# A four-layer attention and time-mix kernel: the steps of the four compute engines placed in another order

## The chip, the core and the metric

The kernel runs on one core of a Trainium2 chip. Its compute engines are TensorE (PE in the profile; its weight loads stand in rows of their own as PEld), VectorE (DVE), ScalarE (ACT) and GpSimd (POOL). SyncE (SP) issues the transfers. Each engine works through its own list of instructions in order and waits at semaphores for what the others make. The metric is the device time of one execution, in microseconds (us), as the median of three runs.

## The reference

`x` has 16 sequences of 128 tokens with 256 channels, and there is a context of the same shape. Four layers follow each other, and each takes the output of the one before:

```python
x = _L0(ctx, x, mask0)    # 16-head attention of x over [ctx, x] (256 keys), RMS norm, 256->1024 GELU ->256
x = _L1(x, ctx, mask1)    # 32-head attention over ctx with 8 kv heads, output product, layer norm
x = _L2(x, state)         # time-mix: token shift, low-rank mixes, then for each of 32 heads of 8x8:
                          #   out = r @ (faaaa * k v^T + s);  s = k v^T + w * s   over 128 tokens
                          # group norm, gate, and a channel-mix of three 256x256 products
x = _L3(x, ctx, mask3)    # 16-head attention of ctx over the layer-normed x, gated output product
```

All of it is in float32.

## The kernel before

The 16 sequences are handled in eight turns of two. The layers of neighbouring turns overlap: the program has phases `@start`, `@first`, `@second`, `@steady0` to `@steady4`, `@closing`, `@last` and `@end`, and a steady phase holds layer 0 of one turn, layers 3 and 2 of the turn before it, and layer 1 of its own turn at the end.

Which engine does which step when is not decided by the code of the steps. Four tables of text, `PE_ORDER`, `ACT_ORDER`, `DVE_ORDER` and `POOL_ORDER`, list the steps of an engine one after the other, and the engine's program walks through its table. A step like `u0`, `q1` or `m2` is one product of 256 channels on PE (L702 and L712) and, on another engine, the emptying of its PSUM bank. `aT`, `yT`, `x1T` are turnings of activations (L693, on PE) and their copies to SBUF.

An attention is cut into jobs of 512 columns: `turn0.7` is the eighth job of layer 0. For each job PE makes the scores of four jobs at once (L757, step `scores`), DVE adds the mask and takes the maximum (L1241), ACT exponentiates (L1064, step `exps`), PE turns the result with four transposes into a PSUM bank (L768, step `turn`), ACT (layers 0 and 3, L1051) or DVE (layer 1, L1257) copies the bank to the buffer `ET`, and PE multiplies that with the values (step `weigh`, L792 for layers 0 and 3, which takes two jobs at once, and L800 for layer 1). A weigh uses PE as four column groups of 32, while turns, products and transposes use the whole array.

Buffers are few. The bank that a turn or a product writes is one of a ring of three (`BANKS = 3`), `E` has two places and `ET` four. So the copy of a job waits for the weigh of the job four before it, by a line in `copy_turned` (L1051 and L1257 stand behind it):

```python
if g >= 4:
    act.wait_ge(sems["pv"], turn("pv", g - 3))
```

The time-mix has a scan over the tokens in eight parts, `vr0` to `vr7`. For each part PE spreads the values (`vp0`, `vp1`), POOL seeds it (`kv<-s,wP`, L1633, step `vr` of POOL_ORDER), DVE multiplies (L1477) and scans (L1484, step `vr` of DVE_ORDER), POOL multiplies with the receptance (`Z`, L1623, step `gather` of POOL_ORDER), and after four such parts PE gathers them (L830, `gather3` and `gather7`). Scan states have two places and `Z` four:

```python
pool.wait_ge(sems["scan"], turn("scan", u - 1))          # seed of part u, from u = 2
dve.wait_ge(sems["z"], turn("z", u - 1))                 # scan of part u, from u = 2
pool.wait_ge(sems["gathered"], turn("gathered", (v - RING_Z) // 4 * 4 + 4))   # Z of part v, from v = 4
```

Of the kernel before, what the change touches and what calls it, by code (L numbers as in the profile page):

```python
# [64 lines left out]
@start xT cT q0 k0l k0c v0c k1 v0l @first aT @start v1 @first scores0.0 turn0.0 turn0.1 scores0.4 turn0.2 weigh0.1  # L65
turn0.3 scores0.8 weigh0.3 cT turn0.4 turn0.5 turn0.6 turn0.7 scores0.12 weigh0.5 turn0.8 weigh0.7 turn0.9 turn0.10
weigh0.9 turn0.11 turn0.12 turn0.13 weigh0.11 turn0.14 turn0.15 weigh0.13 sum0 weigh0.15 o0 nT u0 u1 u2 u3 m2 x1T q1
scores1.0 xT q0 k0l turn1.0 scores1.4 turn1.1 k0c weigh1.0 turn1.2 turn1.3 weigh1.1 v0c weigh1.2 turn1.4 scores1.8
turn1.5 turn1.6 weigh1.3 v0l turn1.7 weigh1.4 weigh1.5 turn1.8 scores1.12 turn1.9 weigh1.6 turn1.10 k1 weigh1.7
turn1.11 weigh1.8 weigh1.9 turn1.12 turn1.13 weigh1.10 weigh1.11 weigh1.12 @second scores0.0 @first turn1.14 turn1.15  # L70
weigh1.13 weigh1.14 @second turn0.0 @first sum1 weigh1.15 v1 @second scores0.4 turn0.1 turn0.2 @first o1 @second
weigh0.1 turn0.3 turn0.4 weigh0.3 scores0.8 turn0.5 turn0.6 turn0.7 scores0.12 weigh0.5 turn0.8 k3 xaT weigh0.7
turn0.9 turn0.10 v3 t turn0.11 mw weigh0.9 turn0.12 turn0.13 mk mv d1 weigh0.11 weigh0.13 k2 v2 turn0.14 turn0.15 d2
sum0 weigh0.15 mr mg o0 r2 vp0 aT g2 nT bonus u0 u1 u2 cT vp1 u3 gather3 m2 gather7 x1T yT q1 xT scores1.0 ynT q0 o2
turn1.0 k0l turn1.1 scores1.4 weigh1.0 k0c xcT weigh1.1 turn1.2 turn1.3 scores1.8 v0c turn1.4 weigh1.2 fk weigh1.3
turn1.5 turn1.6 fr turn1.7 fv weigh1.4 turn1.8 scores1.12 x4T weigh1.5 turn1.9 weigh1.6 weigh1.7 turn1.10 weigh1.8
weigh1.9 q3 turn1.11 weigh1.10 turn1.12 v0l weigh1.11 turn1.13 turn1.14 @steady0 scores0.0 @second weigh1.12 weigh1.13
k1 turn1.15 weigh1.14 sum1 weigh1.15 v1 @steady0 turn0.0 @second o1 @steady0 turn0.1 turn0.2 scores0.4 turn0.3
weigh0.1 turn0.4 weigh0.3 turn0.5 scores0.8 turn0.6 turn0.7 weigh0.5 turn0.8 scores0.12 turn0.9 weigh0.7 turn0.10 xaT
# [5 lines left out]
turn1.12 weigh1.9 weigh1.10 v0l x4T weigh1.11 turn1.13 turn1.14 q3 k1 turn1.15 @steady1 scores0.0 @steady0 weigh1.12
weigh1.13 weigh1.14 sum1 weigh1.15 @steady1 turn0.0 @steady0 o1 @steady1 turn0.1 scores0.4 turn0.2 turn0.3 @steady0 v1
@steady1 weigh0.1 turn0.4 turn0.5 scores0.8 weigh0.3 turn0.6 turn0.7 weigh0.5 turn0.8 scores0.12 turn0.9 xaT weigh0.7
turn0.10 turn0.11 weigh0.9 turn0.12 scores3.0 t turn0.13 weigh0.11 mw mk turn0.14 weigh0.13 d1 mv k2 turn0.15 turn3.0
mr mg v2 turn3.1 d2 scores3.4 sum0 weigh0.15 r2 turn3.2 g2 turn3.3 o0 weigh3.1 vp0 turn3.4 bonus turn3.5 weigh3.3
turn3.6 weigh3.5 k3 nT turn3.7 u0 weigh3.7 u1 sum3 vp1 u2 gather3 u3 o3 m2 gather7 v3 aT yT x1T q1 cT ynT scores1.0 xT  # L90
o2 q0 k0l turn1.0 turn1.1 weigh1.0 scores1.4 turn1.2 xcT k0c weigh1.1 weigh1.2 turn1.3 turn1.4 scores1.8 v0c fk
weigh1.3 turn1.5 weigh1.4 turn1.6 fr fv turn1.7 turn1.8 weigh1.5 v0l scores1.12 turn1.9 x4T weigh1.6 weigh1.7 turn1.10
weigh1.8 weigh1.9 turn1.11 q3 turn1.12 @steady2 scores0.0 @steady1 turn1.13 weigh1.10 turn1.14 weigh1.11 k1 turn1.15
weigh1.12 weigh1.13 weigh1.14 sum1 weigh1.15 v1 @steady2 turn0.0 @steady1 o1 @steady2 turn0.1 scores0.4 turn0.2
turn0.3 weigh0.1 turn0.4 turn0.5 scores0.8 weigh0.3 turn0.6 weigh0.5 turn0.7 turn0.8 scores0.12 xaT turn0.9 weigh0.7
turn0.10 turn0.11 weigh0.9 scores3.0 turn0.12 turn0.13 t weigh0.11 weigh0.13 mw mk turn0.14 d1 mv turn0.15 d2 k2 v2
turn3.0 mr mg scores3.4 turn3.1 r2 sum0 weigh0.15 turn3.2 turn3.3 o0 g2 weigh3.1 turn3.4 turn3.5 bonus weigh3.3 vp0
weigh3.5 nT k3 turn3.6 turn3.7 u0 u1 u2 vp1 weigh3.7 sum3 u3 v3 gather3 m2 gather7 o3 aT yT x1T q1 cT ynT xT scores1.0
o2 q0 k0l turn1.0 scores1.4 turn1.1 turn1.2 k0c xcT weigh1.0 weigh1.1 weigh1.2 turn1.3 v0c turn1.4 scores1.8 fk
turn1.5 fr turn1.6 fv weigh1.3 weigh1.4 turn1.7 turn1.8 scores1.12 x4T weigh1.5 turn1.9 weigh1.6 weigh1.7 turn1.10  # L100
weigh1.8 weigh1.9 q3 turn1.11 turn1.12 v0l weigh1.10 weigh1.11 turn1.13 turn1.14 @steady3 scores0.0 @steady2 k1
turn1.15 weigh1.12 weigh1.13 weigh1.14 sum1 weigh1.15 @steady3 turn0.0 @steady2 o1 @steady3 scores0.4 turn0.1 @steady2
v1 @steady3 turn0.2 turn0.3 weigh0.1 turn0.4 weigh0.3 turn0.5 turn0.6 scores0.8 weigh0.5 turn0.7 turn0.8 scores0.12
xaT turn0.9 weigh0.7 turn0.10 weigh0.9 turn0.11 scores3.0 turn0.12 turn0.13 t weigh0.11 turn0.14 mw mk mv turn0.15
weigh0.13 turn3.0 k2 sum0 d1 v2 weigh0.15 d2 turn3.1 mr mg scores3.4 turn3.2 r2 turn3.3 o0 g2 weigh3.1 turn3.4 turn3.5
vp0 bonus nT weigh3.3 turn3.6 k3 turn3.7 u0 u1 weigh3.5 weigh3.7 sum3 u2 vp1 u3 gather3 v3 m2 gather7 o3 yT aT x1T q1
cT ynT scores1.0 xT q0 o2 turn1.0 turn1.1 scores1.4 turn1.2 k0l k0c turn1.3 xcT weigh1.0 weigh1.1 weigh1.2 turn1.4
scores1.8 turn1.5 v0c turn1.6 weigh1.3 weigh1.4 fk fr weigh1.5 fv turn1.7 turn1.8 weigh1.6 x4T scores1.12 turn1.9
turn1.10 weigh1.7 turn1.11 q3 weigh1.8 turn1.12 weigh1.9 turn1.13 k1 v0l weigh1.10 turn1.14 weigh1.11 weigh1.12
# [1651 lines left out]
```

## Time and profile before

| | us |
|---|---|
| median of three runs (1122.0 to 1125.25) | 1123.47 |
| span of the profiled execution | 1119.7 |
| PE busy, 7776 matmuls | 973.4 (87%) |
| DVE busy | 817.1 (73%) |
| ACT busy | 733.0 (65%) |
| POOL busy | 256.2 (23%) |

The profile is of one execution, whose span is 3.8 us under the median of the runs. Five steady turns of some 126 us each make up the middle; start and tail are emptier. A busy time says how long an engine ran instructions, not whether the others waited for it: for that one reads the chain of waits that ended last, and the idle time ahead of a line with what released it.

### The profile page before, as it was taken

To read this page: it belongs to the slowest core of one execution; us is meant where nothing else is said; L and a number is where in the kernel's file an instruction comes from. 1 tells how busy PE (TensorE), PEld (TensorE's weight loads), DVE (VectorE), ACT (ScalarE), POOL (GpSimd) and SP (SyncE) were. 2 spreads that over 40 slices of the span, in tenths; PEclk is the share of its full clock that TensorE was granted. 3 is DMA by queue.
4 is the path that set the end of the run, shared out by engine and by line. 5 is a ranking of instruction groups with operands and counts; after the bars stand their busy time and mean duration, and the time that the engine had idled before them with its cause. 6 is when DMAs were issued, how large, how long until landed. Compare 5 with 4: busy or idle time off the path is not lost.

```text
span 1119.7 us, 23998 instructions
## 1 busy us (share of the span) xinstructions
PE 973.4 (87%) x7776; PEld 700.2 (63%) x7776; DVE 817.1 (73%) x3119; ACT 733.0 (65%) x2663; POOL 256.2 (23%) x349
## 2 busy tenths in 40 slices
PE   6779898999989899999989899989989899878365
PEld 4456566667767577756766576656766577555243
DVE  3608768977878776987878677977878687876624
ACT  2629852888568883898477882888658883882115
POOL 3210314121411332131411413031321313120300
PEclk9989999999999999999999999999999999899568
DMA  8100000000010001000010001000010000000000
...
DMA packets 18667, 18.90 MB, mean 17 GB/s; under 512 B 7280, under 2 KB 16752, under 8 KB 18288
## 3 DMA queue, kind: packets, MB, share of 16 engines
...
## 4 chain that ended last, share of the span: by engine, by line
PE 47%; ACT 14%; DVE 13%; issue 7%; POOL 2%; DMA 0%; DVEq 0%; POOLq 0%; ACTq 0%
PE ring L702 10%; PE ring L712 10%; ACT E L1064 9%; PE ring L768 8%; PE psS L757 4%; DVE SS L1484 3%; PE ring L933 2%; DVE S L1241 2%; PE psO L800 2%; PE ring L693 2%; PE psO L792 2%; POOL Z L1623 2%; DVE kv L1477 1%; PE psO L830 1%; PE ring L923 1%
## 5 line engine op out<-in xcount | busy, mean ns | idle before, releaser
L1064 ACT ACTIVATE E<-S,nmax 128x128 f32<-128x128 f32 (+1 forms) x1024 | 423.6, 418 | 33.1 <-PE ring L768 22.1
L1241 DVE CUSTOM_DVE_ANT_0 S<-psS,mb 128x128 f32<-128x128 f32 (+1 forms) x1024 | 261.8, 319 | 30.5 <-PE psS L757 15.1
L702 PE MATMUL ring<-slot,w_l 128*128 128x256 f32 x992 | 244.2, 393 | 18.2 <-ACT slot L1025 14.6
L768 PE MATMUL ring<-ident,E 128*128 128x128 f32 x1280 | 200.0, 286 | 45.4 <-ACT E L1064 35.6
L702 PEld LDWEIGHTS ring<-slot,w_l 128*128 128x128 f32 x992 | 185.9, 195 | 57.5 <-ACT slot L1025 17.3
L768 PEld LDWEIGHTS ring<-ident,E 128*128 128x128 f32 x1280 | 142.9, 143 | 120.3 <-ACT E L1064 79.1
L1064 ACT ACTIVATION_READ_ACCUMULATOR E<-S,nmax 128x1 f32 x1024 | 195.7, 191 | 0.0
L712 PE MATMUL ring<-w_l,slot 128*128 128x256 f32 (+1 forms) x640 | 151.6, 381 | 10.9 <-DVE slot L1505 3.5
L712 PEld LDWEIGHTS ring<-w_l,slot 128*128 128x128 f32 x640 | 114.4, 194 | 37.3 <-issue 7.5
L1257 DVE COPY ET<-ring 128x512 f32<-128x512 f32 x140 | 93.2, 685 | 31.9 <-PE ring L768 31.5
L1051 ACT ACTIVATE ET<-ring 128x512 f32<-128x512 f32 x180 | 100.3, 588 | 21.2 <-PE ring L768 20.1
L1484 DVE TENSOR_TENSOR_SCAN SS<-wP,kv 128x258 f32<-128x258 f32 x128 | 105.4, 863 | 5.7 <-POOL Z L1623 3.6
L757 PE MATMUL psS<-keys,slot 32*128 32x512 f32 (+1 forms) x768 | 95.1, 575 | 11.0 <-DVE nmax L1241 5.6
L1025 ACT ACTIVATE slot<-ring 128x512 f32<-128x512 f32 x72 | 42.6, 594 | 76.0 <-PE ring L693 57.8
L693 PE MATMUL ring<-ident,slot 128*128 128x128 f32 x384 | 63.0, 290 | 27.9 <-DVE slot L1217 7.1
L1623 POOL TENSOR_TENSOR Z<-SS,slot 128x512 f32<-128x512 f32 x64 | 79.1, 1237 | 28.0 <-DVE SS L1484 19.1
L1241 DVE DVE_READ_ACCUMULATOR2_ANT nmax<- 128x1 f32 x1024 | 85.5, 83 | 0.0
L1595 POOL TENSOR_TENSOR keys<-k0T,in 128x512 f32<-128x512 f32 x32 | 32.9, 1040 | 222.2 <-PE psS L757 215.1
L693 PEld LDWEIGHTS ring<-ident,slot 128*128 128x128 f32 x384 | 44.2, 146 | 52.2 <-issue 13.1
L792 PE MATMUL psO<-ET,V 128*32 128x128 f32 x1536 | 64.0, 283 | 4.7 <-ACT ET L1051 3.3
L1633 POOL TENSOR_TENSOR kv<-s,wP 128x4 f32<-128x4 f32 x64 | 13.2, 214 | 203.4 <-ACT slot L1025 130.5
L1441 DVE SCALAR_TENSOR_TENSOR slot<-ring,colt,slot 128x256 f32<-128x256 f32 x80 | 34.9, 478 | 32.8 <-PE ring L933 32.7
...
## 6 DMA issues: line engine op xcount, KB each, us to landing
...
```

Of the source, the lines that this page charges most:

```text
L693: m = pe.transpose(b[:, c, a * P:(a + 1) * P], src[:, a, c * P:(c + 1) * P], ident[:, :])
L702: m = pe.matmul(b[:, a, :], w[:, k, m0 + a * P:m0 + (a + 1) * P], src[:, k, :], start=(k == 0), stop=(k == kt - 1))
L712: m = pe.matmul(b[:, bb, 0:n], src[:, k, bb * P:(bb + 1) * P], w[:, k, :], start=(k == 0), stop=(k == kt - 1))
L757: ins = pe.matmul(psS[m % QUAD][:, x * w:(x + 1) * w], queries, keys[rows, group % RING_K, x * w:(x + 1) * w], start=True, stop=True)
L768: m = pe.transpose(b[:, k, :], E[:, g % RING_E, k * P:(k + 1) * P], ident[:, :])
L792: m = pe.matmul(psO[32 * c:32 * c + 32, t, bb * P:(bb + 1) * P], v[:, window(8 * t + 4 * half + c, half, 16)], e, start=(half == 0 and sbl ...
L1051: act.activation(ET[:, g % 4, :, :], bank(phase, i, turned).rearrange("p a (h s) -> p (a h) s", h=2), ACT.Copy).then_inc(sems["emptied_A"], 1)
L1064: ins = act.activation(E[:, g % RING_E, h * w:(h + 1) * w], S[:, g % RING_S, h * w:(h + 1) * w], ACT.Exp, bias=nmax[:, g % 4, h:h + 1], sc ...
L1241: ins = dve.tensor_tensor_reduce(S[:, g % RING_S, h * w:(h + 1) * w], psS[g % QUAD][:, h * w:(h + 1) * w], bias[:, bb, :], -1.0, HUGE, ALU ...
L1257: dve.tensor_copy(ET[:, g % 4, :, :], bank(phase, i, turned).rearrange("p a (h s) -> p (a h) s", h=2))\
L1484: ins = dve.tensor_tensor_scan(SS[:, u % 2, a, :, :].rearrange("p b t -> p (b t)"), wP[:, ct, :, :].rearrange("p b t -> p (b t)"), kv[:, u ...
L1623: pool.tensor_tensor(Z[:, v % RING_Z, :, :].rearrange("p a (b t) -> p a b t", b=PAIR), SS[:, v % 2, :, :, 0:P], r, ALU.mult).then_inc(sems ...
```

## The change

The four tables are written anew, and nothing else is. The tiles, buffers, transfers, the queue of SP and the bodies of the steps are the same; each engine has the same steps as before in another order, and line numbers behind the tables are two lower (L798 after is L800 before). The diff consists of the tables alone, of which one pair of lines, the end of steady0's scan in `PE_ORDER`, is shown:

```diff
-weigh3.5 turn3.6 u0 turn3.7 u1 vp1 weigh3.7 sum3 u2 u3 gather3 o3 m2 gather7 v3 yT aT x1T q1 cT ynT scores1.0 xT o2 q0
+weigh3.5 weigh3.7 vp1 sum3 u2 u3 gather3 o3 m2 gather7 v3 yT x1T aT q1 ynT cT xT scores1.0 q0 o2 scores1.4 turn1.0 k0l
```

On PE the weighs stand together more often. In the layer 1 attention of steady0, from the transposes ahead of one `scores` on, PE had this (L800 is the weigh of layer 1, four instructions for one job; L768 the turn of a job; L757 scores; L712, L693 and L702 products and transposes of other layers):

```order
L768 MATMUL ring<-ident,E 128x128 x4
L800 MATMUL psO<-ET,V 32x128 x8
L757 MATMUL psS<-keys,slot 128x512 x4
L768 MATMUL ring<-ident,E 128x128 x4
L712 MATMUL ring<-w_l,slot 128x256 x4
L768 MATMUL ring<-ident,E 128x128 x4
L800 MATMUL psO<-ET,V 32x128 x4
L768 MATMUL ring<-ident,E 128x128 x4
L800 MATMUL psO<-ET,V 32x128 x8
L712 MATMUL ring<-w_l,slot 128x256 x4
L693 MATMUL ring<-ident,slot 128x128 x4
L800 MATMUL psO<-ET,V 32x128 x4
```

In its place there is now:

```order
L766 MATMUL ring<-ident,E 128x128 x4
L755 MATMUL psS<-keys,slot 128x512 x4
L798 MATMUL psO<-ET,V 32x128 x16
L766 MATMUL ring<-ident,E 128x128 x4
L710 MATMUL ring<-w_l,slot 128x256 x4
L766 MATMUL ring<-ident,E 128x128 x8
L710 MATMUL ring<-w_l,slot 128x256 x4
L691 MATMUL ring<-ident,slot 128x128 x4
L798 MATMUL psO<-ET,V 32x128 x8
```

The weighs that stood in four places, of two, one, two and one job, are now in two, of four and of two jobs, and more turns stand ahead of them.

In the layer 0 attention of steady1 (L792 is the weigh of layers 0 and 3, eight instructions for two jobs) PE had:

```order
L792 MATMUL psO<-ET,V 32x128 x8
L768 MATMUL ring<-ident,E 128x128 x8
L792 MATMUL psO<-ET,V 32x128 x8
L768 MATMUL ring<-ident,E 128x128 x4
L757 MATMUL psS<-keys,slot 128x512 x4
L768 MATMUL ring<-ident,E 128x128 x4
L693 MATMUL ring<-ident,slot 128x128 x4
L792 MATMUL psO<-ET,V 32x128 x8
L768 MATMUL ring<-ident,E 128x128 x8
L792 MATMUL psO<-ET,V 32x128 x8
L768 MATMUL ring<-ident,E 128x128 x4
```

and now has, in the same attention:

```order
L766 MATMUL ring<-ident,E 128x128 x4
L790 MATMUL psO<-ET,V 32x128 x8
L766 MATMUL ring<-ident,E 128x128 x12
L755 MATMUL psS<-keys,slot 128x512 x4
L691 MATMUL ring<-ident,slot 128x128 x4
L766 MATMUL ring<-ident,E 128x128 x8
L790 MATMUL psO<-ET,V 32x128 x16
L755 MATMUL psS<-keys,slot 128x256 x8
```

A pair of jobs was weighed about once in every two turns; two pairs now stand together, behind up to five turns. Counted over the whole program, PE comes to a run of weighs (one or more on end, with nothing between) 168 times before, and 113 times now; of these 60, 80 and 28 were in layers 0, 1 and 3, and are 42, 50 and 21. All changes of PE between the whole array, column groups (weighs, gathers) and row groups (scores, spreads and others) are 578 before and 460 now. In 49 places of the program the turn of a job now stands ahead of the weigh that empties its place of `ET`; before there was no such place. From the end of such a turn to the end of that weigh PE has work of 0.8 us in the mean, and 38 us in all, counted with the durations of the steps in the trace of before.

On POOL the seeds and the `Z` of the scan stand in groups. In the scan of steady0, POOL had (L1633 `kv` is a seed, L1623 `Z` the multiplication):

```order
L1633 TENSOR_TENSOR kv<-s,wP 128x4
L1623 TENSOR_TENSOR Z<-SS,slot 128x512
L1633 TENSOR_TENSOR kv<-s,wP 128x4
L1623 TENSOR_TENSOR Z<-SS,slot 128x512
L1633 TENSOR_TENSOR kv<-s,wP 128x4
L1623 TENSOR_TENSOR Z<-SS,slot 128x512 x3
```

as the end of a list in which the two alternate, and now has, for the whole scan behind its first three seeds:

```order
L1621 TENSOR_TENSOR Z<-SS,slot 128x512 x2
L1631 TENSOR_TENSOR kv<-s,wP 128x4 x2
L1621 TENSOR_TENSOR Z<-SS,slot 128x512 x2
L1631 TENSOR_TENSOR kv<-s,wP 128x4 x3
L1621 TENSOR_TENSOR Z<-SS,slot 128x512 x4
```

Seeds 5, 6 and 7 now stand ahead of `Z` 4, and seed 3 stands behind `Z` 1. The other turns have like groups, not the same ones; steady3 also has a group norm of layer 3's entry (`norm3`) ahead of seed 0.

Around the product `q1`, ACT copied `aT` ahead of `x1T`, which alone `q1` needs, in each steady turn. Now `x1T` is copied ahead of `aT` in steady0 and steady4, and PE has `cT` between `x1T` and `q1` in steady1. In steady2 the order on both engines was `aT`, `yT`, `x1T` and is `yT`, `aT`, `x1T`, which it already was in steady0, steady3 and steady4.

## Rows read from the trace of the kernel before

**Rows 1.** the page's first line and its part 1, busy time of the engines.

```profile
span 1119.7 us, 23998 instructions
...
PE 973.4 (87%) x7776; PEld 700.2 (63%) x7776; DVE 817.1 (73%) x3119; ACT 733.0 (65%) x2663; POOL 256.2 (23%) x349
```

**Rows 2.** the page's part 4, share of the ending chain by engine.

```profile
PE 47%; ACT 14%; DVE 13%; issue 7%; POOL 2%; DMA 0%; DVEq 0%; POOLq 0%; ACTq 0%
```

**Rows 3.** chain by line: end of steady0's layer 0, then its layer 1.

```profile
by line: PE ring L712 34.0%; PE ring L702 33.9%; PE psO L792 8.8%; PE ring L768 7.9%; PE psO L830 5.1%; PE ring L693 4.8%; PE psS L816 4.1%; PE ring L959 4.1%; issue 0.1%
...
by line: ACT E L1064 30.3%; DVE S L1241 11.6%; PE ring L712 10.1%; PE ring L768 10.0%; PE ring L702 7.2%; issue 6.8%; PE psO L800 4.2%; DVE ET L1257 3.6%; PE ring L693 3.0%; DVE slot L1217 2.5%; DVE bst L1205 2.1%; DVE slot L1508 1.7%; DVE 
```

**Rows 4.** busy time by stretch: two steady turns, then the tail.

```profile
300.00:426.50 126.50, 117.50 (x977) 85.55 (x974) 100.56 (x389) 90.97 (x333) 32.60 (x42) 1.00 0.04 10
805.00:932.00 127.00, 117.18 (x987) 85.16 (x987) 102.00 (x389) 91.72 (x334) 30.62 (x40) 1.00 0.04 10
...
1010.00:1080.00 70.00, 41.73 (x206) 27.80 (x207) 41.34 (x68) 10.10 (x21) 12.40 (x18) 0.74 0.01 4
```

**Rows 5.** timeline of PE in steady0's layer 1 attention (start, duration).

```profile
343.87 0.60 PE L768 MATMUL ring<-ident,E 128*128 128x128 f32 x4
344.40 0.64 PE L800 MATMUL psO<-ET,V 128*32 128x128 f32 x16
344.98 1.14 PE L757 MATMUL psS<-keys,slot 32*128 32x512 f32 x8
...
352.80 0.43 PE L800 MATMUL psO<-ET,V 128*32 128x128 f32 x8
353.15 1.09 PE L768 MATMUL ring<-ident,E 128*128 128x128 f32 x8
```

**Rows 6.** timeline of PE around one product in steady2.

```profile
592.10 0.60 PE L768 MATMUL ring<-ident,E 128*128 128x128 f32 x4
592.53 1.89 PE L712 MATMUL ring<-w_l,slot 128*128 128x256 f32 x8
594.35 0.64 PE L800 MATMUL psO<-ET,V 128*32 128x128 f32 x16
```

**Rows 7.** idle time ahead of L792, then ahead of L800.

```profile
  issue: 17.7, 63
...
  issue: 14.2, 60
```

**Rows 8.** timeline of ACT, then PE, around q1 of two turns.

```profile
313.81 1.02 ACT L1036 ACTIVATE slot<-ring,colt 128x256 f32<-128x256 f32 x2
314.71 0.61 ACT L1025 ACTIVATE slot<-ring 128x512 f32<-128x512 f32 x1
...
315.38 1.99 PE L702 MATMUL ring<-slot,w_l 128*128 128x256 f32 x8 [1.70 <-ACT slot L1025]
...
823.18 1.99 PE L702 MATMUL ring<-slot,w_l 128*128 128x256 f32 x8 [1.70 <-ACT slot L1025]
```

**Rows 9.** waits of line L1051, ACT's copies into ET.

```profile
L1051 ACT ACTIVATE ET<-ring x180: 569/592/611, 29.3 to 1110.0; 128x512 f32<-128x512 f32 x180
...
  PE ring L768: 20.1, 27
```

**Rows 10.** scan stage of steady0: POOL, DVE, then waits for L1623.

```profile
300.34 1.49 POOL L1623 TENSOR_TENSOR Z<-SS,slot 128x512 f32<-128x512 f32 x1 [1.09 <-PE psO L830]
...
301.95 1.66 POOL L1623 TENSOR_TENSOR Z<-SS,slot 128x512 f32<-128x512 f32 x1
...
299.57 1.28 DVE L1484 TENSOR_TENSOR_SCAN SS<-wP,kv 128x258 f32<-128x258 f32 x2
...
301.94 2.23 DVE L1484 TENSOR_TENSOR_SCAN SS<-wP,kv 128x258 f32<-128x258 f32 x2 [0.50 <-POOL Z L1623]
...
  PE psO L830: 8.9, 6
...
  PEld psO L830: 13.6, 6
```

More of the change, by code:

```diff
@@ L64 @@
 PE_ORDER = """
[L65 to L79, printed above, removed]
@@ L85 @@
[L85 to L99, printed above, removed]
@@ L100 @@
[L100 to L109, printed above, removed]
@@ new lines @@
+turn1.11 turn1.12 weigh1.9 weigh1.10 weigh1.11 turn1.13 k1 turn1.14 @second scores0.0 @first turn1.15 sum1 v1
+weigh1.12 weigh1.13 weigh1.14 weigh1.15 @second turn0.0 scores0.4 turn0.1 turn0.2 @first o1 @second turn0.3 scores0.8
+turn0.4 weigh0.1 weigh0.3 turn0.5 turn0.6 turn0.7 weigh0.5 scores0.12 turn0.8 k3 xaT turn0.9 weigh0.7 turn0.10 v3 t
+turn0.11 turn0.12 mw weigh0.9 weigh0.11 mk d1 mv turn0.13 k2 turn0.14 turn0.15 v2 sum0 weigh0.13 weigh0.15 mr mg d2 o0
+r2 vp0 aT g2 nT bonus u0 u1 u2 vp1 u3 gather3 cT m2 gather7 x1T yT q1 scores1.0 xT ynT q0 o2 k0l turn1.0 turn1.1
@@ new lines @@
+weigh3.5 turn3.6 u0 turn3.7 u1 weigh3.7 vp1 sum3 u2 u3 o3 gather3 m2 gather7 v3 aT yT x1T cT q1 ynT xT scores1.0 o2 q0
+k0l turn1.0 turn1.1 scores1.4 weigh1.0 turn1.2 xcT k0c turn1.3 v0c scores1.8 weigh1.1 weigh1.2 turn1.4 fk turn1.5
+turn1.6 fr fv weigh1.3 weigh1.4 weigh1.5 turn1.7 turn1.8 v0l turn1.9 scores1.12 x4T turn1.10 weigh1.6 weigh1.7
+weigh1.8 weigh1.9 turn1.11 q3 turn1.12 @steady2 scores0.0 @steady1 turn1.13 weigh1.10 weigh1.11 turn1.14 k1 turn1.15
+weigh1.12 sum1 weigh1.13 weigh1.14 weigh1.15 v1 @steady2 turn0.0 @steady1 o1 @steady2 turn0.1 scores0.4 turn0.2
@@ L131 @@
+weigh3.7 o3
 """
 ACT_ORDER = """
[L134 to L137 removed]
@@ L241 @@
+apply4 shift0 fv @end mask3.0 mask3.1 mask3.2 mask3.3 mask3.4 mask3.5 turn3.1 mask3.6 mask3.7 turn3.3 turn3.5 inv3
+turn3.7 sum3 o3
 """
 POOL_ORDER = """
-@first norm3 scores0.0 scores0.4 scores0.8 scores0.12 @second norm3 @first sum0 scores1.0 hn x1T @second scores0.0
-scores0.4 scores0.8 @first norm1 apply1 norm2 @second sum0 scores0.12 scores1.0 vr0 vr1 hn vr2 gather0 vr3 gather1 vr4
-gather2 vr5 gather3 vr6 gather4 @steady0 norm3 @second vr7 gather5 gather6 gather7 x1T norm4 @steady0 scores0.0
@@ L247 @@
-scores0.4 @second norm1 apply1 @steady0 scores0.8 scores0.12 @second norm2 @steady0 scores3.0 scores3.4 scores1.0 vr0
-vr1 sum0 hn vr2 gather0 vr3 gather1 vr4 gather2 vr5 gather3 vr6 gather4 vr7 gather5 gather6 gather7 x1T @steady1 norm3
-@steady0 norm4 @steady1 scores0.0 scores0.4 @steady0 norm1 apply1 @steady1 scores0.8 scores0.12 @steady0 norm2
-@steady1 scores3.0 scores3.4 scores1.0 vr0 vr1 sum0 hn vr2 gather0 vr3 gather1 vr4 gather2 vr5 gather3 vr6 gather4 vr7
-gather5 gather6 gather7 x1T @steady2 norm3 @steady1 norm4 @steady2 scores0.0 scores0.4 @steady1 norm1 apply1 norm2
@@ L262 @@
-norm4
+@first norm3 sum0 scores0.0 scores0.4 scores0.8 hn scores0.12 scores1.0 x1T @second scores0.0 scores0.4 scores0.8
+@first norm1 apply1 norm2 @second norm3 sum0 vr0 vr1 hn gather0 vr2 vr3 gather1 gather2 vr4 vr5 gather3 gather4 vr6
+vr7 gather5 gather6 gather7 scores0.12 scores1.0 x1T norm4 @steady0 scores0.0 scores0.4 @second norm1 apply1 norm2
+@steady0 scores0.8 norm3 scores0.12 sum0 scores3.0 scores3.4 scores1.0 vr0 vr1 hn vr2 gather0 gather1 vr3 vr4 gather2
+gather3 vr5 vr6 vr7 gather4 gather5 gather6 gather7 x1T norm4 @steady1 scores0.0 scores0.4 scores0.8 @steady0 norm1
@@ L263 @@
+@last scores3.0 @closing x1T @end scores3.0 @closing norm1 apply1 norm2 @last vr0 vr1 vr2 gather0 gather1 vr3 vr4
+gather2 gather3 vr5 vr6 gather4 vr7 gather5 gather6 gather7 norm4
 """
```

303 lines of the change are left out of this document (165 added, 138 removed).

## The prediction

> **What bounds the kernel now.** I read the page first. PE is busy for 973.4 of the 1119.7 us span, DVE for 817.1, ACT for 733.0 and POOL for 256.2 [rows 1], so the first question is whether PE's busy time is the time. The chain of work that ended last says: less than half of it. PE carries 47% of the chain, ACT 14%, DVE 13%, issue 7% [rows 2]. Cut by stretch, the chain looks different in each stage [rows 3]. At the end of layer 0, with its products and the MLP, PE stands alone in it: the two product lines have 34.0% and 33.9% and all other rows of that stretch are PE's too. In the layer 1 attention ACT's exponentials lead with 30.3%, DVE's masking has 11.6%, and PE's rows there (10.1, 10.0, 7.2, 4.2 and 3.0%) add up to 34.5%. The windows give a second measure: in a steady turn PE is busy for 117.50 of 126.50 us, and in the last for 117.18 of 127.00, at a granted clock of 1.00 [rows 4]. So a turn has 9.0 us (126.50 - 117.50) in which PE waits, against 117.5 in which it works. The tail is another matter: 41.73 of 70.00 us at a granted clock of 0.74, one step after the other. What a new order can win in the middle is either some of these 9 us, or PE time that isn't work.
>
> **PE: fewer runs of weighs.** Such time exists. A weigh uses column groups, the steps around it the whole array, and the timeline shows a price for going in and out. Take start to start. A run of one job lasts 0.35 us (352.80 to 353.15), a run of two 0.58 (344.40 to 344.98) [rows 5]; so a job costs 0.23 more in a run and a run 0.12 for itself (0.35 - 0.23). Four transposes last 0.43 ahead of a product (592.10 to 592.53) [rows 6] and 0.53 ahead of a weigh (343.87 to 344.40) [rows 5]: 0.10 more. A product ahead of a weigh takes 1.82 (592.53 to 594.35) [rows 6]. That is some 0.22 for a run, and what follows one may pay a little more. The second way to count agrees: ahead of the weighs of layers 0 and 3 there stand 17.7 us of idle time that nothing shown releases ("issue"), in 63 places, and 14.2 in 60 ahead of layer 1's [rows 7]; (17.7 + 14.2) / 123 = 0.26 for a run. I take 0.26. The change leaves 113 runs where there were 168, so 55 x 0.26 = 14.3 us less PE time (12.1 at 0.22).
>
> The page TensorEngine Tiling (Array Packing) of the Trainium skill, section Key Properties, says that changing the tiling mode, and not just the tile, drains TensorE; the rows agree, with 0.26 us at a run of weighs. By that rule scores and spreads would pay too, and all changes of shape count: 118 fewer (578 to 460) at half of 0.26 make 15.3 us, one more than by the runs.
>
> How much of the 14.3 reaches the end? At most the share of time that PE is busy in a turn, 117.5 / 126.5 = 0.93, if every other engine has room; at least PE's share of the chain, 0.47. Where ACT or DVE leads, a weigh that is done sooner only makes PE wait longer for the next exponentials. I choose 0.6, nearer to the chain, since the runs saved lie in the attentions, where PE has 34.5% of the chain [rows 3], and not in the MLP, where it has all: -8.6 us (bounds -6.7 and -13.3).
>
> **q1.** In steady0 and steady4 PE stands still for 1.70 us ahead of q1, until ACT has copied x1T, and ACT's copies of aT (313.81 to 314.71, 0.90) go first [rows 8]. With x1T ahead of aT this falls by 0.90 in both; aT's reader comes later. In steady1 cT's transposes fill about as much. In steady2 the order becomes that of steady0 before, and gives back up to 0.5. Together -2.0 (0 to -2.7).
>
> **ET.** Before, ACT's copies into ET waited for turns, 20.1 us in 27 places [rows 9], and a weigh held none of them up for long. In 49 places a turn now stands on PE ahead of the weigh that frees its place, 0.8 us of PE work apart, 38 us in all. There the copy can't start when its turn is done, and ACT, or DVE in layer 1, stands with its next exponentials or masks behind it. What covers this is that ACT is mostly late with the copy anyhow, busy with exponentials; only 27 of its 180 copies stood ready and waiting for the turn. If 27/180 of the 38 us are felt, that is 5.7 us of waiting on ACT; times ACT's share in an attention's chain (30.3% [rows 3]) 1.7. I take +2.5, for DVE's part and PE's own stops at the full ring (bounds 0 and 38 x 0.30 = 11.4).
>
> **The scan on POOL.** The parts of the scan run on in DVE, 1.28 us each without a disturbance, and scan 6 waits for Z 4. In steady0 before, scan 5 ended at 300.85 (299.57 + 1.28), Z 4 ran from 300.34 to 301.83, held by PE's gather3, and scan 6 began at 301.94 after 0.50 of waiting [rows 10]. Now seed 7 stands ahead of Z 4, and a seed waits for the scan two parts earlier: scan 5. So Z 4 can't begin before 300.85 + 0.2, and scan 6 not before 302.5: 0.6 later. Where gather3 is not late, it is up to 1.1. PE waits at the gathers for Z in six places, 13.6 us together [rows 10]; six times 0.6 to 1.1 is 3.6 to 6.6, less where other steps of PE now stand ahead of gather7. I take +3.0 (bounds 0 and 8 x 1.1 = 8.8, one for each scan).
>
> **The rest.** Start and tail hold the same instructions with a few neighbours exchanged (v1 behind scores0.0, fk ahead of fr). Nothing in them is removed, and I put them at nothing. SP's queue is the same, and DMA has 0% of the chain [rows 2], so steps that are moved past transfers don't count.
>
> **The sum.** -8.6 - 2.0 + 2.5 + 3.0 = -5.1 us; 1119.7 - 5.1 = 1114.6 as a span. The median of the runs lies 3.8 above the profiled span (1123.47 - 1119.7), so 1118.4, and I predict 1118. No change and a change of less than 0.3% (3.4 us, 1120.1 to 1126.8) can't be told apart by a measurement.
>
> **Rivals.**
> *All of the 14.3 us arrives.* For it: PE is busy for 93% of a turn, and ACT for 91 of 126.50 us [rows 4], so it has room. -13.3 - 2.0, and the holds on ET and the scan covered to a half, +2.8: -12.5, 1111; with nothing held, 1108. Against it: PE has only 34.5% of the chain where most runs are saved.
> *No change.* PE's saved time turns into waits for exponentials in the attentions. Then only the third of it counts that PE has of the chain there (14.3 x 0.345 = -4.9), -2.0 for q1, and +6 for ET and scan: -0.9, 1122.5. For it: ACT's lead in rows 3. Against it: more turns in a row let ACT and DVE run further ahead.
> *Slower: the scan becomes the bound.* Grouped seeds and Z's put scan 6, and with it gather7, o2 and all that follow, 1.1 later in each of eight turns (+8.8), and gather7's wait grows also by what PE arrives earlier, so that of the 8.6 about half is lost there (+4.3), with ET's holds at twice my value (+5): 10.6 gained and 18.1 lost, +7.5, 1131. It decides from the point where scan and ET together cost over 10.6 us, twice my 5.5. Against it: two thirds of PE's time at those gathers can be filled with the MLP's products, u2 to m2, which stand there.
> The change does what its tables say, as the lists of instructions show; that it doesn't is no case.
>
> **Chances.** My forecast (1113 to 1120) has 0.44, all arriving 0.17, no change 0.22, slower 0.17. Faster by over 0.3% is the first two, 0.61; within it 0.22; slower 0.17. The range takes in the full gain at 1108 with some of the unknown (ET's lower bound, q1's upper), and of the slower case the nearer half: 1106 to 1129. The likeliest case's own range is 1113 to 1120.
>
> **What would show it.** Right: in the profile after, the idle time by "issue" ahead of the weighs falls to about 113/168 of 31.9 us, 21; PE's busy time falls by most of the 14.3, since the rows of the timeline run into each other and the price lies within them; a steady turn ends some 1 us sooner, its 9.0 us of PE waiting grown by a little; q1's wait falls to about 0.8 in steady0 and steady4. ACT's copies into ET would list weighs as a releaser, for some us; scan 6 would list Z with more than the 0.50 of steady0. Wrong: if the turns are as long as before and ACT's exponentials wait longer for turns, or if PE's waits at the gathers exceed 13.6 us by more than 6, the price of the grouping is larger than the price of the switches. If issue falls and PE's busy time doesn't, the switch cost PE nothing.

## The result, and the profile after

The changed kernel takes 1102.93 us (median of four runs, 1100.49 to 1105.67), against 1123.47 us for the kernel before (a fourth run of that one, of 5128.6 us, is left out): a ratio of 0.9824, with a 95% interval of 0.9802 to 0.9847. A second job (a session on the chip in which the kernel before is timed again; this one is e13) gave 1100.8 us and 0.9806 (0.9779 to 0.9833). So the change is 20 to 21 us faster, where 5 were forecast, and lies under the forecast's range.

The page's first line and its busy times, which answer to [rows 1]:

```profile
span 1103.7 us, 23998 instructions
...
PE 963.7 (87%) x7776; PEld 709.8 (64%) x7776; DVE 825.9 (75%) x3119; ACT 730.0 (66%) x2663; POOL 259.5 (24%) x349
```

In this execution, the slowest of the four, PE's busy time fell by 9.7 us (973.4 to 963.7), and the time in which PE waits fell by 6.3: 146.3 us before (1119.7 - 973.4), 140.0 now. The page of e13, the same kernel:

```profile
span 1098.6 us, 23998 instructions
...
PE 958.5 (87%) x7776; PEld 706.6 (64%) x7776; DVE 824.6 (75%) x3119; ACT 730.0 (66%) x2663; POOL 260.0 (24%) x349
```

There PE is busy for 14.9 us less than before and waits for 140.1 (1098.6 - 958.5), 6.2 less. The mean granted clock of TensorE was 0.963 in it, 0.955 in the slower execution and 0.966 in the kernel before. The forecast was that PE's busy time falls by 14.3 and its waits grow: by 5.7 (14.3 - 8.6), and with q1, ET and the scan, which are waits too, by 9.2 in all (5.7 - 2.0 + 2.5 + 3.0). The first came out; the second went the other way.

The idle time ahead of the weighs that nothing shown releases, first of layers 0 and 3, then of layer 1, which answers to [rows 7]:

```profile
  issue: 11.9, 50
...
  issue: 11.1, 40
```

It fell from 31.9 us in 123 places to 23.0 in 90; 21 was expected. The waits for turns say more. First the kernel before: who waited for a turn (L768), us and times.

```profile
  DVE ET L1257: 31.5, 39
  ACT E L1064: 22.1, 30
```

And the changed kernel (L766):

```profile
  ACT ET L1049: 20.3, 22
  ACT E L1062: 17.0, 18
  DVE ET L1255: 13.3, 24
```

DVE's copies of layer 1 wait 13.3 us for turns, not 31.5, and the exponentials 17.0, not 22.1. ACT's copies wait as long as before (20.1 in [rows 9]). The copies into ET, which answer to [rows 9], ACT's and then DVE's:

```profile
  PE ring L766: 20.3, 22
  PE psO L790: 3.9, 3
...
  PE ring L766: 13.3, 24
  PE psO L790: 5.1, 3
  PE psO L798: 2.0, 4
```

The holds that the prediction named (copies into ET that stand until a weigh has emptied their place) are there: 3.9 us on ACT and 7.1 on DVE are waits for weighs. The scan, which answers to [rows 10], shows who waits for PE's gather and for Z:

```profile
  PE psO L828: 5.1, 3
...
  PEld psO L828: 14.6, 7
  PE psO L828: 13.3, 7
  DVE SS L1482: 7.6, 9
```

Scans wait 7.6 us for Z, twice the 3.6 of before, and PE's loads at the gathers 14.6, where [rows 10] have 13.6.

For the next table the eight turns were cut at PE's first instruction of scores0.0, o0 and q1, as PE's timeline gives them, and the stretches of one kind added up (PE's waiting in brackets). The last two columns are the experiments e9 and e10 below.

| us (of it PE waits) | before | after | e9 | e10 |
|---|---|---|---|---|
| layer 0 attention, scores0.0 to o0 | 363.7 (41.0) | 357.4 (36.8) | 373.6 (44.7) | 367.2 (45.8) |
| MLP and scan, o0 to q1 | 281.9 (23.4) | 286.6 (29.4) | 289.9 (30.9) | 284.9 (27.5) |
| layer 1 attention, q1 to the next scores0.0 | 319.0 (23.2) | 306.0 (18.1) | 321.9 (24.5) | 319.4 (29.1) |
| start and tail | 151.7 (55.3) | 150.3 (52.4) | 151.1 (55.8) | 151.5 (55.8) |

The gain lies in the attentions, 19.3 us in both kinds, and in layer 1 above all; 9.3 of the 19.3 are waits of PE (4.2 and 5.1). The stretch with the scan lost 4.7.

### The profile page after: what moved, and what is told of

The parts are those of the page before. It is cut to its first block and busy times, and to the rows that moved or that the text cites. A ratio compares the mean times of both kernels' runs of the same rounds, so it can differ in the third digit from the quotient of the medians.

```text
span 1103.7 us, 23998 instructions
## 1 busy us (share of the span) xinstructions
PE 963.7 (87%) x7776; PEld 709.8 (64%) x7776; DVE 825.9 (75%) x3119; ACT 730.0 (66%) x2663; POOL 259.5 (24%) x349
## 5 line engine op out<-in xcount | busy, mean ns | idle before, releaser
L766 PE MATMUL ring<-ident,E 128*128 128x128 f32 x1280 | 197.7, 286 | 31.5 <-ACT E L1062 28.5
L700 PEld LDWEIGHTS ring<-slot,w_l 128*128 128x128 f32 x992 | 189.1, 198 | 53.0 <-ACT slot L1023 15.0
L766 PEld LDWEIGHTS ring<-ident,E 128*128 128x128 f32 x1280 | 145.1, 144 | 104.6 <-ACT E L1062 68.8
L1049 ACT ACTIVATE ET<-ring 128x512 f32<-128x512 f32 x180 | 99.6, 588 | 24.5 <-PE ring L766 20.3
L1255 DVE COPY ET<-ring 128x512 f32<-128x512 f32 x140 | 92.5, 683 | 20.7 <-PE ring L766 13.3
L755 PE MATMUL psS<-keys,slot 32*128 32x512 f32 (+1 forms) x768 | 98.6, 581 | 7.9 <-ACT ET L1049 2.0
L1023 ACT ACTIVATE slot<-ring 128x512 f32<-128x512 f32 x72 | 42.5, 592 | 74.7 <-PE ring L691 59.7
L1621 POOL TENSOR_TENSOR Z<-SS,slot 128x512 f32<-128x512 f32 x64 | 76.5, 1202 | 57.6 <-DVE SS L1482 52.4
L790 PE MATMUL psO<-ET,V 128*32 128x128 f32 x1536 | 61.4, 291 | 2.0 <-ACT ET L1049 1.7
L710 PE MATMUL ring<-w_l,hT 128*128 128x256 f32 x256 | 57.1, 381 | 0.9 <-ACT hT L1034 0.9
L1153 ACT ACTIVATE slot<-ring 128x512 f32<-128x512 f32 x8 | 4.8, 598 | 79.8 <-PE ring L969 79.8
```

The costliest lines, as they stand in the source:

```text
L700: m = pe.matmul(b[:, a, :], w[:, k, m0 + a * P:m0 + (a + 1) * P], src[:, k, :], start=(k == 0), stop=(k == kt - 1))
L710: m = pe.matmul(b[:, bb, 0:n], src[:, k, bb * P:(bb + 1) * P], w[:, k, :], start=(k == 0), stop=(k == kt - 1))
L755: ins = pe.matmul(psS[m % QUAD][:, x * w:(x + 1) * w], queries, keys[rows, group % RING_K, x * w:(x + 1) * w], start=True, stop=True)
L766: m = pe.transpose(b[:, k, :], E[:, g % RING_E, k * P:(k + 1) * P], ident[:, :])
L790: m = pe.matmul(psO[32 * c:32 * c + 32, t, bb * P:(bb + 1) * P], v[:, window(8 * t + 4 * half + c, half, 16)], e, start=(half == 0 and sbl ...
L1049: act.activation(ET[:, g % 4, :, :], bank(phase, i, turned).rearrange("p a (h s) -> p (a h) s", h=2), ACT.Copy).then_inc(sems["emptied_A"], 1)
```

## The experiments

Each was timed in five rounds against the kernel before, except the probe (e12). The change itself is 0.9824 and 0.9806 of the kernel before on this scale, in its two jobs. Theory A: a run of weighs costs PE a fixed time, and the change gains by having fewer. Theory B: the order of all steps to each other is what it gains by. Theory C: holds on ET and the grouped scan take part of the gain back.

**Fewer runs alone, in two directions.** In e1 a run of weighs waits for the next one, in e2 it joins the one ahead. Only weighs are moved.

```diff
 e1 (PE_ORDER, @first)
-scores0.4 turn0.2 weigh0.1 turn0.3 scores0.8 weigh0.3 cT turn0.4
+scores0.4 turn0.2 turn0.3 scores0.8 weigh0.1 weigh0.3 cT turn0.4
 e2 (PE_ORDER, @first)
-scores0.12 weigh0.5 turn0.8 weigh0.7
+scores0.12 weigh0.5 weigh0.7 turn0.8
```

> The kernel before, with 53 of its runs of weighs put off until the next run (past at most four other steps), so that PE comes to 115 runs where it had 168; all other steps keep their order, and ACT, DVE and POOL have the tables of before. Turns, scores and products come sooner by it, and 61 turns now stand ahead of the weigh that frees their place of ET. Theory A (a run of weighs costs PE 0.2 to 0.26 us, nearly all of which reaches the end): PE's busy time falls by 10 to 14 us, and the kernel takes 1110 to 1114 us. Theory B (what counts is that turns come ahead of weighs, so that E is free sooner and ACT's exponentials start sooner): 1105 to 1112 us, and ACT waits less for turns than the 22.1 us ahead of the exponentials of before. Theory C (the prediction's cost of the holds on ET): the gain is given back by more than 5 us in ACT's and DVE's copies, 1116 to 1122 us.

> The kernel before, with 54 runs of weighs pulled ahead to the run before them (past at most five other steps), so that PE comes to 114 runs; nothing else is moved, and no turn stands ahead of the weigh that frees its place of ET. Turns, scores and products come later by it. Theory A: as many runs are saved as in the other direction, so PE's busy time falls by 10 to 14 us and the kernel takes 1110 to 1114 us, as with the weighs put off. Theory B: the turns come later and PE stands at weighs whose copies are not done, so the saving is lost: 1120 to 1130 us. Theory C: without holds on ET it is the better of the two, by 5 us or more.

Measured: e1 1152.68 us, 1.0260 of before (1.0242 to 1.0277); e2 1163.53 us, 1.0354 (1.0339 to 1.0369). Both are far slower, though they save as many runs as the change does, so A and B both missed; C was too low for e1, and had e2 the better of the two, which it isn't. PE's busy time did not fall by 10 to 14 us either: it is 973.0 us in e1 and 989.5 in e2, against 973.4, at a mean granted clock of 0.961 and 0.949 in these two executions, against 0.966. The copies of e1 show one cause. ACT's waits, then DVE's:

```profile
  PE psO L792: 21.7, 11
...
  PE psO L800: 14.6, 11
```

36.3 us of copies wait for weighs at 61 holds, where the change has 11.0 at 49. In e2 there are no holds, but PE stands at its weighs until the copies of the same jobs are made (before, PE's matmuls waited so for 3.3 us at the weighs of layers 0 and 3, and not at those of layer 1):

```profile
PE psO L791 <- ACT ET L1050: 17.6, 19, 2.6
...
PE psO L799 <- DVE ET L1256: 13.0, 13, 2.5
```

**More runs, in the changed kernel.** e3 puts the last weigh of a run off past one step in 70 places, e5 pulls the first one ahead of one step in 49.

```diff
 e3 (PE_ORDER, @first)
-turn0.5 weigh0.1 weigh0.3 turn0.6 turn0.7
+turn0.5 weigh0.1 turn0.6 weigh0.3 turn0.7
 e5 (PE_ORDER, @steady0)
-weigh1.9 turn1.10 fv turn1.11 turn1.12 v0l x4T weigh1.10 weigh1.11
+weigh1.9 turn1.10 fv turn1.11 turn1.12 v0l weigh1.10 x4T weigh1.11
```

> The changed kernel, with the last weigh of a run put off past one other step in 70 places, so that PE comes to 183 runs of weighs where the change has 113; nothing else is moved. Theory A: 70 runs more at 0.2 to 0.26 us make PE's busy time 14 to 18 us longer, and the kernel takes 1115 to 1120 us. Theory B: turns and products come no later than in the change, so the time stays within 4 us of it, 1101 to 1107 us.

> The changed kernel, with the first weigh of a run pulled ahead of the one step in front of it in 49 places: 162 runs of weighs where the change has 113, and 31 turns ahead of the weigh that frees their place of ET instead of 49. In the split the other way 70 runs more cost 16 us, 0.23 each. Theory A (each run of weighs costs 0.2 to 0.26 us, whichever way it is split): 10 to 13 us more than the change, 1113 to 1116 us. Theory B (what counts is what stands ahead of what): the turns come later here and the weighs sooner, the reverse of the other split, so that the time comes out otherwise by 5 us or more; with fewer holds on ET it could be 1103 to 1108 us.

Measured: e3 1119.17 us, 0.9961 (0.9948 to 0.9973): 16.2 us more than the change, 0.23 for each run, as A had it. e5 1108.75 us, 0.9870 (0.9851 to 0.9888): 5.8 us more, 0.12 for each run, half of A's, with 18 fewer holds. In e3 PE is busy for 14.1 us longer than in e13's execution of the change, whose granted clock is near its own (0.963 and 0.960), and waits 6.5 longer: its page has a span of 1119.2 us with 972.6 of busy PE, so that PE waits 146.6 us against 140.1. So 0.20 us a run is busy time, and the rest of the loss is waits.

**The scan's grouping.** e4 is the change with the seeds and Z of before.

```diff
 (POOL_ORDER, @steady0, the scan's steps)
-vr0 vr1 vr2 gather0 gather1 vr3 vr4 gather2 gather3 vr5 vr6 vr7 gather4
+vr0 vr1 vr2 gather0 vr3 gather1 vr4 gather2 vr5 gather3 vr6 gather4 vr7
```

> The changed kernel, with the seeds and the Z of each scan on POOL in the alternating order of before (in the same places of POOL's table). The prediction's term (the grouping puts Z 4 behind seed 7 and costs 3.0 us in all, at most 8.8): 1094 to 1100 us. Its rival (the groups cost nothing, since PE's and DVE's other work covers them): within 2 us of the change, 1101 to 1105 us.

Measured: 1103.14 us, 0.9813 (0.9798 to 0.9828), the same as the change. If the grouping costs something at the end, it is within the noise of some 2 us; nothing of the prediction's +3.0 shows.

**ET with eight places.** In e6 the change has them, in e7 the kernel e1.

```diff
-        ET = sb("ET", [4, 4, P])
+        ET = sb("ET", [8, 4, P])
...
-                    if g >= 4:
-                        act.wait_ge(sems["pv"], turn("pv", g - 3))
+                    if g >= 8:
+                        act.wait_ge(sems["pv"], turn("pv", g - 7))
```

> The changed kernel with eight places of ET where it has four; no order is changed, and a copy waits for the weigh of the job eight before it. The 49 holds on ET fall away. If the holds cost the change something (the prediction put +2.5 us, at most 11.4; the trace after lists 11.0 us of copies that wait for weighs): 1097 to 1101 us. If they lie beside other waits: within 2 us of the change, 1101 to 1105 us.

> The kernel before with 53 runs of weighs put off (as in the run that came to 1152.68 us) and with eight places of ET. In that run copies waited 36.3 us for weighs (21.7 on ACT, 14.6 on DVE) at 61 holds. If the holds are what made it slow, and a run of weighs costs 0.23 us: the 36 us go and the 53 runs saved show, 12 us less than the kernel before, 1108 to 1114 us. If something else is late in it (scores, other products, values): 1125 to 1150 us.

Measured: e6 1100.67 us, 0.9811 (0.9786 to 0.9836), 2.3 us under the change's first job and level with its second, so the holds cost the change 0 to 2.3 us. e7 comes to 1127.31 us, 1.0031 (1.0014 to 1.0048): the holds made 25.4 of the 29 us that e1 loses. But without them, 53 runs fewer still gain nothing: the second of the two cases named ahead. PE's busy time in e7 is 967.0 us, 6.4 less than before, and its waiting grew by 11.3 ((1124.6 - 967.0) - 146.3).

**Weighs and all other steps apart.** The turns have the same order in both kernels, so a weigh has a place among them in each. e9 has all other steps from the change and the weighs among the turns as before; e10 is the converse; e11 is e10 with eight places of ET. A few weighs (one group of four jobs in e9, two in e10) keep their kernel's own place.

```diff
 e9 against the change (PE_ORDER, @first)
-scores0.4 turn0.2 turn0.3 cT turn0.4 scores0.8 turn0.5 weigh0.1 weigh0.3 turn0.6
+scores0.4 turn0.2 weigh0.1 turn0.3 weigh0.3 cT turn0.4 scores0.8 turn0.5 turn0.6
 e10 against the kernel before (PE_ORDER, @first)
-scores0.4 turn0.2 weigh0.1 turn0.3 scores0.8 weigh0.3 cT turn0.4 turn0.5 turn0.6
+scores0.4 turn0.2 turn0.3 scores0.8 cT turn0.4 turn0.5 weigh0.1 weigh0.3 turn0.6
```

> All steps but the weighs stand as in the changed kernel (ACT, DVE, POOL and PE's turns, scores and products), and PE's weighs stand among the turns where they stood before: 167 runs of weighs instead of 113, and 4 holds on ET instead of 49. If the fewer runs are what the change gains by (theory A, 0.12 to 0.23 us a run by the two splits): 54 runs more cost 6 to 12 us, 1109 to 1115 us. If the order of all other steps is what it gains by (theory B): within 3 us of the change, 1100 to 1106 us. If the weighs' places are all of it: 1120 to 1125 us.

> The converse: all steps but the weighs stand as in the kernel before, and PE's weighs stand among the turns where the change has them: 115 runs instead of 168, 46 holds on ET instead of none. Theory A: 1110 to 1117 us. Theory B (the other steps are what counts, and the weighs' new places only fit them): as slow as the mechanical merging, 1140 to 1155 us, with copies that wait for weighs.

> The run before it with eight places of ET, so that no copy waits for a weigh. Theory A: 53 runs saved without a hold, 1110 to 1117 us. Theory B: like the mechanical merging with eight places, 1120 to 1130 us, since weighs that stand later than the order of before provides for delay the emptying that follows them.

Measured: e9 1141.9 us, 1.0156 (1.0135 to 1.0178); e10 1130.84 us, 1.0057 (1.0038 to 1.0075); e11 1130.96 us, 1.0074 (1.0047 to 1.0100). No theory had e9; e10 lies between the ranges of A and B, and e11 just above B's. e11 is level with e10, so it isn't the holds that e10 loses by. The new order of everything else, with the old weighs, is 17 us slower than the kernel before; the new weighs, with the old order of everything else, are 6 us slower; both together are 20 us faster. The page of e9, and how long DVE's copies waited for its turns:

```profile
span 1139.8 us, 23998 instructions
...
PE 980.6 (86%) x7776; PEld 704.7 (62%) x7776; DVE 824.1 (72%) x3119; ACT 733.5 (64%) x2663; POOL 259.2 (23%) x349
...
  DVE ET L1255: 28.0, 34
```

Against the change PE is busy for 16.9 us longer (980.6 - 963.7, 0.31 for each of 54 runs) and waits 19.2 longer ((1139.8 - 980.6) - 140.0). The same of e10:

```profile
span 1126.3 us, 23998 instructions
...
PE 964.8 (86%) x7776; PEld 702.5 (62%) x7776; DVE 818.3 (73%) x3119; ACT 732.5 (65%) x2663; POOL 256.0 (23%) x349
...
  DVE ET L1257: 27.7, 33
```

Against the kernel before PE is busy for 8.6 us less and waits 15.2 longer ((1126.3 - 964.8) - 146.3). In both, DVE's copies wait some 28 us for turns; in the change it is 13.3.

Waits are not the whole of e9. It has as many runs of weighs as the kernel before (167 and 168), and yet PE is busy for 7.2 us longer (980.6 - 973.4), besides 12.9 of waits ((1139.8 - 980.6) - 146.3). The mean granted clock is 0.954 to 0.956 in its five executions and 0.962 to 0.968 in those of the kernel before beside it; in e10 it is 0.962 to 0.969. So part of e9's loss, by this estimate some 7 us, is the same matmuls at a lower clock. Which of e9's waits bring the lower clock was not traced.

**The price of a run by itself.** e12 adds blocks behind the kernel's last product, so that its time says nothing of the change; nothing in the blocks waits for another engine, and what they compute goes nowhere.

```diff
+                for n in range(24):
+                    probe_turn(n)
+                for each, run in ((probe_turn, 1), (probe_turn, 2), (probe_turn, 4), (probe_turn, 24), (probe_product, 1),
+                                  (probe_product, 4), (probe_product, 24)):
+                    for m in range(0, 24, run):
+                        for n in range(m, m + run):
+                            each(n)
+                        for n in range(m, m + run):
+                            probe_weigh(n)
```

> The kernel before, and behind its last product on PE, which nothing waits for, blocks of 24 turns (four transposes each) and 24 weighs of one job (four matmuls each), in runs of 1, 2, 4 and 24, and then 24 products of four matmuls with 24 weighs in runs of 1, 4 and 24. Nothing in the blocks waits for another engine. By the timeline of before a run of weighs costs 0.22 to 0.26 us on PE: the block of 24 runs takes 5.1 to 6.0 us more than that of one run, for turns and for products. By the split kernels' busy time it would be 0.13 us, 3.0 us more.

PE's timeline in the blocks of turns (L1015) and weighs (L1019): start, duration, then the number of matmuls.

```profile
1150.52 0.66 PE L1015 MATMUL psS<-ident,E 128*128 128x128 f32 x4
...
1151.46 0.66 PE L1015 MATMUL psS<-ident,E 128*128 128x128 f32 x4
...
1159.73 1.09 PE L1015 MATMUL psS<-ident,E 128*128 128x128 f32 x8
...
1161.33 1.09 PE L1015 MATMUL psS<-ident,E 128*128 128x128 f32 x8
...
1172.52 1.97 PE L1015 MATMUL psS<-ident,E 128*128 128x128 f32 x16
...
1175.42 1.96 PE L1015 MATMUL psS<-ident,E 128*128 128x128 f32 x16
...
1189.95 10.70 PE L1015 MATMUL psS<-ident,E 128*128 128x128 f32 x96
...
1205.96 0.92 PE L1024 MATMUL psS<-slot,w_l 128*128 128x256 f32 x3
```

Start to start, a turn and a weigh take 0.94 us in runs of one (1150.52 to 1151.46), 0.80 in runs of two (1.60 from 1159.73 to 1161.33), 0.73 in runs of four (2.91 / 4) and 0.67 in runs of 24 (1189.95 to 1205.96, 16.01 / 24). From one to two the run costs (0.94 - 0.80) x 2 = 0.28 us, and from two to four (0.80 - 0.73) x 4 = 0.28. The block of 24 runs takes 6.5 us more than that of one, (0.94 - 0.67) x 24, where 5.1 to 6.0 were expected. With products (L1024):

```profile
1208.24 1.99 PE L1024 MATMUL psS<-slot,w_l 128*128 128x256 f32 x8
...
1210.52 1.99 PE L1024 MATMUL psS<-slot,w_l 128*128 128x256 f32 x8
...
1260.68 7.17 PE L1024 MATMUL psS<-slot,w_l 128*128 128x256 f32 x32
...
1268.80 7.17 PE L1024 MATMUL psS<-slot,w_l 128*128 128x256 f32 x32
```

A product and a weigh take 2.28 us in runs of one and 2.03 (8.12 / 4) in runs of four: (2.28 - 2.03) x 4 / 3 = 0.33 for a run. So PE pays 0.28 to 0.33 us for each run of weighs where nothing else holds it up, and the prediction's 0.26 was a little low. In the kernels less of it comes out: PE's busy time is 8.6 us less in e10 and 6.4 in e7, for 53 runs, 0.16 and 0.12 each. Why isn't shown.

**q1.** e8 restores the order around q1 in three turns; after e8 had come out 5 us faster than the change's first job, e13 repeated the change beside e14 and e15, which each restore one half, and e16, which has all of q1's old order and eight places of ET.

```diff
 e14 (and e8): PE_ORDER, @steady0; ACT_ORDER, @steady0 and @steady4
-x1T aT
+aT x1T
 e15 (and e8): PE_ORDER, @steady1
-cT q1 ynT
+q1 cT ynT
```

> The changed kernel with aT again ahead of x1T (in steady0 on PE and ACT, in steady4 on ACT) and with cT behind q1 in steady1. The prediction's term (0.9 us in each of three turns): 2.0 to 2.7 us more than the change, 1105 to 1106 us. Its rival (the time before q1 is given back at ynT, which waits for DVE anyway): within 1 us of the change.

> The changed kernel once more, as the measure for the three runs beside it: 1101 to 1105 us by the earlier runs of it.

> The changed kernel with aT again ahead of x1T in steady0 (PE and ACT) and steady4 (ACT); cT stays ahead of q1 in steady1. By the prediction (0.9 us won in each of two turns): 1.8 us slower than the change in this job. If the time won at q1 is lost again at the next wait: the same within 1 us. If the earlier run's 5 us are real and lie here: 2 to 5 us faster.

> The changed kernel with cT again behind q1 in steady1 and nothing else. By the prediction (cT's transposes fill the wait): up to 0.9 us slower than the change in this job. If cT only delays q1, ynT and what follows: 1 to 2 us faster.

> The changed kernel with q1's old order in all three turns and with eight places of ET. If the two earlier runs (1098.05 and 1100.67 us) hold and add up, 1095 to 1097 us, 6 to 8 us under the change in this job. If the first was a matter of its job: 2 to 3 us under the change.

Measured: e8 1098.05 us, 0.9774 (0.9755 to 0.9793), faster than either of its cases had it; in the later job e13 1100.8, e14 1102.06, 0.9804 (0.9774 to 0.9833), e15 1097.91, 0.9782 (0.9754 to 0.9810), e16 1097.47, 0.9768 (0.9740 to 0.9796). x1T ahead of aT gains at most the 1.3 us of e14 over e13, which is within their spread. cT ahead of q1 loses: the three kernels without it (e8, e15, e16) are at 1097.5 to 1098.1, and those with it (both jobs of the change, e4, e6, e14) at 1100.7 to 1103.1. The intervals of e13 and e15 overlap, but PE's rows show where the time goes. e13, the change: PE's timeline from cT, then the window of 433.5 to 437.3 us (the last columns are the granted clock, DMA share and GB/s).

```profile
433.46 0.66 PE L691 MATMUL ring<-ident,slot 128*128 128x128 f32 x4 [2.51 <-DMA slot<-in_ctx]
433.95 3.48 PE L700 MATMUL ring<-slot,w_l 128*128 128x256 f32 x8
...
433.50:437.30 3.80, 3.80 (x13) 2.98 (x14) 1.84 (x3) 0.28 (x1) 0.32 (x1) 0.58 0.33 106
```

cT waits 2.51 us for the transfer of a context that has not landed yet, and q1 stands behind it. Then PE's granted clock is 0.58 in the window behind the wait, and q1's product (433.95) takes 3.48 us instead of 1.99. With cT behind q1 again (e15: q1, ynT and xT, and the same window):

```profile
432.25 1.99 PE L700 MATMUL ring<-slot,w_l 128*128 128x256 f32 x8 [1.23 <-ACT slot L1023]
...
435.22 0.66 PE L691 MATMUL ring<-ident,slot 128*128 128x128 f32 x4 [0.55 <-DVE slot L1498]
436.79 0.66 PE L691 MATMUL ring<-ident,slot 128*128 128x128 f32 x4 [0.91 <-DMA slot<-in_x]
...
433.50:437.30 3.80, 2.35 (x16) 1.65 (x14) 2.96 (x6) 1.37 (x3) 0.40 (x1) 1.00 0.34 106
```

PE has three shorter waits, 1.23, 0.55 and 0.91, the clock is 1.00, and q1's product starts 1.70 us sooner and takes 1.99. By the scores of the next layer 0 attention that leaves e15 1.24 us ahead; then e13 has a second stretch at a low clock. e13's scores, the third turn behind them and a window; then the scores and the turn of e15:

```profile
497.87 1.15 PE L755 MATMUL psS<-keys,slot 32*128 32x256 f32 x16 [1.95 <-ACT ET L1049]
...
503.47 0.66 PE L766 MATMUL ring<-ident,E 128*128 128x128 f32 x4
...
500.00:505.00 5.00, 5.00 (x37) 3.24 (x37) 2.18 (x16) 3.48 (x10) 0.40 (x1) 0.76 0.00 0
...
496.63 1.15 PE L755 MATMUL psS<-keys,slot 32*128 32x256 f32 x16 [1.96 <-ACT ET L1049]
...
500.57 0.66 PE L766 MATMUL ring<-ident,E 128*128 128x128 f32 x4
```

From the scores to that turn e13 takes 5.60 us and e15 3.94, behind a wait of the same length; e15's granted clock is 1.00 there. That puts e15 2.90 us ahead, as much as the medians differ. Why the clock fell behind that wait in e13 and not in e15 isn't shown. e16 differs from e8 by the eight places of ET alone and is 0.6 us faster, so the holds cost the change little, if anything. e16 is the fastest kernel of the study, 24.7 us under the kernel before, but not clear of e15 and e8.

## Why the prediction was wrong

**What bounds the kernel** was read rightly: PE's time in the attentions has a part that isn't work, and the change takes it out. But of the two things that a new order can win by its own words, "some of these 9 us" in which PE waits and PE time that isn't work, it gave the first no term but q1's.

**The price of a run** was right in mechanism and close in size: 0.26 forecast, 0.28 to 0.33 in the probe, and 55 runs at 0.28 are 15.4 us; e13's busy time fell by 14.9. Whether scores and spreads pay likewise, as the prediction's 15.3 us have it, no run measured.

**How much of it reaches the end** is the step that failed: "I choose 0.6, nearer to the chain, since the runs saved lie in the attentions". It took the rest of the order as given, and from it that the time saved would turn into waits for ACT and DVE. Where the rest is as given, that was even too kind. In e10, e11 and e7 the runs are saved, PE is busy for less, and its waits grow by 11 to 15 us, more than it saved. In the change PE's waits shrank by 6.2 to 6.3, where the forecast had them grow, because the other steps stand where they fit the later weighs: with the other steps of before, the same places of the weighs lose (e10). e9 shows that the new places of the other steps are no gain by themselves either. So the share that reaches the end was not between 0.47 and 0.93 by the chain or the busy share; counted this way it is under zero or over one, by whether the other steps follow.

**ET**: +2.5 forecast, 0 to 2.3 measured (e6). That the same holds can cost much was not in its range: in e1 they cost 25 us (e7), where copies stood 36.3 us for weighs. The bound "38 x 0.30 = 11.4" was for the change's own table, where it held.

**The scan**: +3.0 forecast, nothing seen (e4). Z 4 is later, as the 7.6 us of waiting scans show, but the alternating order gives no time back at the end.

**q1**: -2.0 forecast. The waits fell as said, 1.70 to 0.79 in steady0 and steady4 of the changed kernel. In steady0 PE's next wait tells what became of the time. The change, q1 and then ynT (the transposes that wait for DVE), and behind them the same of e14, with the old order:

```profile
310.07 1.99 PE L700 MATMUL ring<-slot,w_l 128*128 128x256 f32 x8 [0.79 <-ACT slot L1023]
313.95 0.33 PE L691 MATMUL ring<-ident,slot 128*128 128x128 f32 x1 [1.89 <-DVE slot L1498]
...
309.85 1.99 PE L700 MATMUL ring<-slot,w_l 128*128 128x256 f32 x8 [1.70 <-ACT slot L1023]
312.83 1.81 PE L691 MATMUL ring<-ident,slot 128*128 128x128 f32 x12 [0.98 <-DVE slot L1498]
```

Both orders wait 2.68 us in all: what q1 wins, ynT gives back. And cT, which was to fill a wait, brought one of 2.51 us for a transfer and two stretches at a low clock: some 3 us lost (e13 and e15). The sentence that failed there is "steps that are moved past transfers don't count": the transfers were the same, but a step that needs one was moved ahead of its landing.

**The sum** with what was measured: -15.4 for the runs, 0 to +2.3 for ET, 0 for the scan, +1.6 to +2.9 for q1 (2.9 from e15 against e13, less the 1.3 of e14) give -10.2 to -13.8. The change gained 20 to 21. The 6 to 11 us that are left lie with PE's waits in the attentions, 9.3 us less in the table above, which the prediction had as a cost. e13's page says it without the single terms: PE's busy time fell by 14.9 us for 14.3 forecast, and its waits fell by 6.2 where 9.2 more were forecast. The prediction's rival "all of the 14.3 us arrives" came nearest, at 1108 to 1111.

**What stays open**: which moves of the other steps, on PE or on ACT and DVE, make the new weighs fit. The four tables hold each other's order through the ring of three banks, and no run exchanged one engine's table alone but POOL's scan (e4). In e9 and e10 a weigh has its place among the turns; where it stands among the steps between two turns had to be chosen anew, and no other choice was run. That DVE's copies wait 13.3 us for turns in the change and 28 in e9 and e10 says in which stage it lies, not by which step. How much of e1, e2 and e9 is the lower granted clock, and how much the waits themselves, is told only roughly.
